# A graph-transformer layer on one core: block counts and the filter pipeline's first products moved within the prologue

## What is computed

```python
xn = _layernorm(x, axis=-1)
x = x + gnn(xn, src, dst, edge_attr_20, edge_weight, edge_attr_3, ...) + attention(xn[None], Wq, Wk, Wv, Wo, bo)[0]
x = x + experts(_layernorm(x, axis=-1)[None], ...)[0]

# gnn, for every edge
xs = x[:, :C] @ (W_in2f_s / sqrt(C));  xv = einsum(x[:, C:], W_in2f_v) / sqrt(C)   # the node table
h = softplus(f_ij @ Wf1 + bf1) - LOG2                                              # f_ij: 20 features of the edge
W = (h @ Wf2 + bf2) * rcut_ij[:, None]                                             # the edge's filter
agg = segment_sum(messages(xs[idx_j], xv[idx_j], direction, W), idx_i)

# attention, 8 heads: softmax over q and k, context = k^T v, out = q context
v = x @ Wv;  q = softmax(x @ Wq);  k = softmax(x @ Wk)
```

## Time and profile before

| | us |
|---|---|
| median of 3 runs | 1355.48 |
| lowest and highest | 1350.85, 1355.99 |
| the profiled execution, its own time | 1353.98 |
| its span | 1352.2 |
| PE, DVE, ACT, POOL busy in the span | 1222.9, 1077.6, 824.4, 846.0 |
| mean granted clock of TensorE | 0.958 of 2.4 GHz |

### The profile page before, as it was taken

How to read it: one execution, slowest core, us unless ns; L and a number is a source line. 1 busy time by engine, 2 the same in 40 slices (tenths; PEclk the granted TensorE clock), 3 DMA queues, 4 the chain that set the end, 5 groups by cost and what they waited for, 6 DMA issues and landing times.

```text
span 1352.2 us, 16153 instructions
## 1 busy us (share of the span) xinstructions
PE 1222.9 (90%) x4175; PEld 709.1 (52%) x4175; DVE 1077.6 (80%) x2018; ACT 824.4 (61%) x1821; POOL 846.0 (63%) x785
## 2 busy tenths in 40 slices
PE   5989999999999998799999999999979999977993
PEld 3566666667776663334343343434434444766870
DVE  5868888899999994788889888898968887577325
ACT  3677777767777641566666666667655774774320
POOL 7167777777777775667676767777675881051215
PEclk8989999999999998899999999999999999978995
DMA  9147776778779857878788888888787881645447
GB/s 267 54 148 274 283 285 233 276 274 307 277 290 340 283 206 276 308 266 288 268 292 280 281 284 283 283 286 299 265 278 249 304 275 38 205 173 167 162 120 231
DMA packets 103663, 336.58 MB, mean 249 GB/s; under 512 B 16260, under 2 KB 17196, under 8 KB 94228
## 3 DMA queue, kind: packets, MB, share of 16 engines
q0 software_dynamic: 56896, 186.92, 39.1%
q1 hardware_dynamic: 46676, 148.63, 31.9%
HBM read 211.34 MB, written 124.14 MB: 248 GB/s over the span
## 4 chain that ended last, share of the span: by engine, by line
PE 63%; DVE 15%; ACT 7%; issue 6%; DMA 5%; POOL 3%; DVEq 1%; SPq 0%; POOLq 0%; ACTq 0%
PE PS L2147 16%; PE PS L2152 13%; PE PS L2083 11%; PE PS L2274 6%; ACT RR L1136 4%; PE PS L1971 3%; PE PS L1961 3%; DVE RR L1627 3%; PE PS L1943 2%; DVE RR L1467 2%; PE PS L2042 2%; DMA RR<-node_table,RR 2%; DVE RR L1647 1%; POOL RR L941 1%; DMA X<-in_x 1%
## 5 line engine op out<-in xcount | busy, mean ns | idle before, releaser
L1136 ACT ACTIVATE RR<-RR 128x256 f32<-128x256 f32 x966 | 394.2, 494 | 245.5 <-PE PS L2152 202.2
L891 POOL DMA_INDIRECT RR<-node_table,RR x322 | 426.0, 1323 | 182.5 <-ACT RR L1136 81.3
L857 POOL DMA_INDIRECT edge_records<-RR x316 | 319.9, 1012 | 115.4 <-issue 67.7
L2147 PE MATMUL PS<-RR 128*125 128x512 f32 x644 | 302.6, 614 | 36.8 <-DVE RR L1627 27.9
L2152 PE MATMUL PS<-RR 128*125 128x512 f32 x644 | 289.6, 592 | 0.0
L2147 PEld LDWEIGHTS PS<-RR 128*125 128x125 f32 x644 | 121.3, 193 | 209.9 <-issue 203.8
L2152 PEld LDWEIGHTS PS<-RR 128*125 128x125 f32 x644 | 120.9, 188 | 155.7 <-issue 155.7
L1467 DVE TENSOR_TENSOR RR<-PS,RR 128x512 f32<-128x512 f32 x237 | 161.0, 686 | 29.9 <-PE PS L2083 28.3
L2083 PE MATMUL PS<-wf_high,h_high 128*128 128x512 f32 x316 | 146.6, 464 | 1.6 <-ACT RR L1090 1.5
L1627 DVE TENSOR_TENSOR RR<-RR 128x1536 f32<-128x1536 f32 (+1 forms) x81 | 140.9, 1740 | 0.0
L2083 PE MATMUL PS<-wf_high,h_low 128*128 128x512 f32 x316 | 125.2, 396 | 0.0
(11 more groups left out here) (340 smaller groups left out, 1828.6 us busy)
## 6 DMA issues: line engine op xcount, KB each, us to landing
RR<-edge_records SPq DMA_DIRECT2D x73, 1040.0 KB, 6.2
expert_inputs<-RR SPq DMA_DIRECT2D x8, 2560.0 KB, 14.2
RR<-in_L_ffn_beta_w SPq DMA_DIRECT2D x8, 1024.0 KB, 7.2
expert_w_raw<-in_L_ffn_expert_w SPq DMA_DIRECT2D x8, 1024.0 KB, 7.5
expert_outputs<-RR SPq DMA_DIRECT2D x27, 256.0 KB, 2.0
RR<-edge_records SPq DMA_DIRECT2D x10, 520.0 KB, 4.4
edge_records<-RR POOLq DMA_INDIRECT x322, 3.9
RR<-node_table,RR POOLq DMA_INDIRECT x322, 5.0
```

The source lines that it names most:

```text
L857: g.indirect_dma_start(out=rec_dram, out_offset=place, in_=ST[:, j, :], in_offset=None).then_inc(scattered[c], 16)
L891: g.indirect_dma_start(out=GB[:, q % GBS, t, 1:5, :].rearrange("p k n -> p (k n)"), out_offset=None, in_=tab_dram, in_offset=bass.Indirect ...
L1136: last = a.activation(message_slot(q)[:, t, k:k + 5:4, :], GB[:, q % GBS, t, 0:k + 3:k + 2, :], ACT.Copy, scale=record_slot(q)[:, t, 4 * C ...
L2147: te.matmul(PS[0:NT, 2 * (r % PSS), :], OH[:, q % OHS, t, 0:NT], GB[:, q % GBS, t, 1:5, :].rearrange("p k n -> p (k n)"), start=(n == 0), ...
```

## The change

It moves instructions and changes two PSUM banks; no instruction is added or removed.

- DVE: `count_block(1)` and `(2)` stand ahead of the wait for the deviations of tiles 2 and 3, `(3)` and `(4)` a place earlier, `(5)`, `(6)` and `(7)` ahead of the wait for those of tiles 6 to 9, `(8)` and `(9)` between the normalisations of tiles 6, 7 and 8.
- PE: the count products stand behind value product 5 instead of 7 (`COUNT_TILE`). Table product 9 and value products 8 and 9 are taken out of the loop and stand between the filter pipeline's first transposes and first layer. The waits for all copies of the prologue stand where their banks are first used again.
- The bias product L2055 writes bank 5 instead of 3, since bank 3 is still in use by value product 8.
- ACT: the rounding of the weights and the first two `stage_f` come a tile earlier; the copies follow PE's new order, and `log_part(0, 0)` stands ahead of the copy of value product 9.
- DVE at the head of the loop: `low(0, 0)` stands ahead of `hidden(0, 1)`.

```diff
@@ -582,7 +582,7 @@
 
             return 4 * (t % 2)
 
-        COUNT_TILE = 7
+        COUNT_TILE = 5
         TILE_STEP, PER = 3, 6
         CTX_STEP = TILE_STEP + PER * NB - 1
         WO_STEP = CTX_STEP + 2
@@ -1024,10 +1024,13 @@
             values(1)
             moments_of((5,))
             later_std(slice(4, 6), 5)
-            for t in range(2, NB):
+            def bias_rows():
+                act.wait_ge(b2_psum, 1)
+                a.activation(b2_rows, PS[:, 5, :], ACT.Copy).then_inc(b2_ready, 1)
+
+            for t in range(2, NB - 1):
                 table_rows(t)
-                if t + 1 < NB:
-                    evac_xT(t + 1)
+                evac_xT(t + 1)
                 if t < 4:
                     moments_of((2 * t + 2, 2 * t + 3))
                 if t == 3:
@@ -1035,8 +1038,9 @@
                     act.wait_ge(nrm_sq, 1)
                     a.activation(inv, ssq, ACT.Sqrt).then_inc(nrm_root, 1)
                     a.preload_act_table_set("natural_log_exp_and_others")
-                values(t)
-                if t == 5:
+                if t < NB - 2:
+                    values(t)
+                if t == 4:
                     act.wait_ge(consts, 3)
                     a.activation(ones2[:, :], two_rows, ACT.Copy)
                     a.activation(ident_r[:, :], ident[:, :], ACT.Copy).then_inc(w_rounded, 1)
@@ -1046,12 +1050,9 @@
                     a.activation(wf2_high[:, :, :], wf2[:, :, :], ACT.Copy).then_inc(w_rounded, 1)
                     stage_f(0)
                     stage_f(1)
-                if t == 7:
+                if t == 6:
                     act.wait_ge(w_ordered, 2)
                     a.activation(b2hl[0:2, :], b2f, ACT.Copy).then_inc(w_rounded, 1)
-
-            act.wait_ge(b2_psum, 1)
-            a.activation(b2_rows, PS[:, 3, :], ACT.Copy).then_inc(b2_ready, 1)
 
             def radial(i, c):
 
@@ -1110,13 +1111,17 @@
                 if 0 <= t < NB and r == 3:
                     exp_k(t)
 
+            bias_rows()
+            table_rows(NB - 1)
             radial(0, 0)
             stage_f(2)
+            values(NB - 2)
+            log_part(0, 0)
             radial(0, 1)
-            log_part(0, 0)
-            log_part(0, 1)
             high(0, 0)
             stage_f(3)
+            values(NB - 1)
+            log_part(0, 1)
             radial(0, 2)
             stage_f(4)
             radial(0, 3)
@@ -1398,21 +1403,26 @@
             dve.wait_ge(edge_in, 16 * 6)
             receiving_blocks()
             count_block(0)
+            count_block(1)
+            count_block(2)
             inverse_root(range(2, 4), 1)
             normal(2)
             normal(3)
-            count_block(1)
-            count_block(2)
+            count_block(3)
             inverse_root(range(4, 6), 2)
             normal(4)
-            count_block(3)
+            count_block(4)
             normal(5)
-            count_block(4)
+            count_block(5)
+            count_block(6)
+            count_block(7)
             inverse_root(range(6, NB), 3)
-            for t in range(5, NB):
-                if t + 1 < NB:
-                    normal(t + 1)
-                count_block(t)
+            normal(6)
+            count_block(8)
+            normal(7)
+            count_block(9)
+            normal(8)
+            normal(9)
             dve.wait_ge(w_rounded, 4)
             stage_f_low(0, 0)
             stage_f_low(0, 1)
@@ -1579,10 +1589,10 @@
 
             stage_f_low(0, 2)
             hidden(0, 0)
-            hidden(0, 1)
-            stage_f_low(0, 3)
             dve.wait_ge(b2_ready, 1)
             low(0, 0)
+            stage_f_low(0, 3)
+            hidden(0, 1)
             stage_f_low(0, 4)
             dve.wait_ge(dirs_ready, 1)
             dve.wait_ge(v_psum, NB)
@@ -1920,9 +1930,8 @@
 
             transpose_x(0)
             transpose_x(1)
-            for t in range(NB):
-                if t == 2:
-                    transpose_x(2)
+
+            def table_product(t):
                 pe.wait_ge(xT_ready, t + 1)
                 if t == 0:
                     pe.wait_ge(wsv_in, 32)
@@ -1933,8 +1942,7 @@
                                      start=True, stop=True)
                 last.then_inc(tab_psum, 1)
 
-                if 2 <= t < NB - 1:
-                    transpose_x(t + 1)
+            def value_product(t):
                 if t == 0:
                     pe.wait_ge(wqkv_in[2], 32)
                 elif t >= 2:
@@ -1943,15 +1951,19 @@
                     last = te.matmul(PS[0:NT, 3 + t % 2, :], XTQ[:, t, k, :], WV[:, k, :], start=(k == 0),
                                      stop=(k == KD - 1))
                 last.then_inc(v_psum, 1)
+
+            for t in range(NB - 1):
+                if t == 2:
+                    transpose_x(2)
+                table_product(t)
+                if t >= 2:
+                    transpose_x(t + 1)
+                if t < NB - 2:
+                    value_product(t)
                 if t == COUNT_TILE:
                     pe.wait_ge(counts_ready, NB)
                     te.matmul(PS[:, 7, 0:NB], ltri[:, :], cnt, start=True, stop=True)
                     te.matmul(PS[:, 7, NB:2 * NB], ones[:, 0:P], cnt, start=True, stop=True).then_inc(counts_psum, 1)
-
-            pe.wait_ge(counts_read, 1)
-            pe.wait_ge(xT_ready, NB)
-            pe.wait_ge(tab_ready, NB)
-            pe.wait_ge(v_ready, NB)
 
             def query(t, k):
                 if k == 0 and t == 0:
@@ -2052,15 +2064,21 @@
 
 
             pe.wait_ge(w_rounded, 5)
-            te.matmul(PS[:, 3, :], ones2[:, :], b2hl[:, :], start=True, stop=True).then_inc(b2_psum, 1)
+            te.matmul(PS[:, 5, :], ones2[:, :], b2hl[:, :], start=True, stop=True).then_inc(b2_psum, 1)
+            table_product(NB - 1)
             transposes(0, 0)
-            transposes(0, 1)
+            value_product(NB - 2)
             pe.wait_ge(wf2_l, 1)
             layer1(0, 0)
+            transposes(0, 1)
+            value_product(NB - 1)
+            pe.wait_ge(tab_ready, NB)
             layer1(0, 1)
             transposes(0, 2)
+            layer1(0, 2)
             transposes(0, 3)
-            layer1(0, 2)
+            pe.wait_ge(counts_read, 1)
+            pe.wait_ge(v_ready, NB)
 
             pe.wait_ge(b2_ready, 1)
             pe.wait_ge(wf2_l, 2)
```

## The result

| | before | changed |
|---|---|---|
| median of 11 runs, us | 1353.2 | 1347.4 |
| lowest and highest, us | 1350.35, 1356.16 | 1338.79, 1350.19 |
| profiled execution: own time, span, us | 1353.98, 1352.2 | 1342.33, 1340.6 |
| mean granted clock | 0.958 | 0.964 |

The ratio of the times is 0.9951, with a 95% interval of 0.993 to 0.9972: 3.8 to 9.5 us less, 6.6 in the middle, against the forecast 3.9. The profiled execution is 11.6 us shorter than the one before, much more than the forecast, so the first question is where in the span these 11.6 us lie.

The account below looks back on a forecast made before the run. PE is busy 90%, but at 70 to 81 us serial ACT and DVE latency leaves it waiting. 4.2 gained less 0.3 for count blocks gives 3.9 us: 1350.1, or 1351.6 against the median; range 1346.5 to 1356.

Parts of the forecast that it names:

- The walk along PE: Prologue tail on PE: one pause of 2.5 us instead of 6.4 in four; step 0 at 75.8, gaining 4.7.
- The step on the clock: Steps 0 and 1: gain 6.4 us if the clock holds through the pause, 4.2 if it falls.
- I take the fall: Pause before step 0: clock assumed to fall, as after three of five similar later pauses; gain 4.2 us.
- Step 0 then costs what it costs today: Step 0 after a clock fall: lasts as before, 7.40 us, instead of about 5.7 at full clock.
- by the same amount: Filter steps behind step 1: POOL's last scatter comes earlier by the whole head start, 4 to 6 us.
- the five pauses behind 590 us: Later PE pauses of 2.57 to 2.67 us: each may lose or keep its clock anew, a fall costing 1.7 us.
- The count blocks: DVE ahead of tile 2: two count blocks fill the 4.59 us wait, delaying it by 0.3 us.
- the slower rival: Count blocks run into POOL before tile 2: PE 6.3 us later, result 1357.6; chance 0.08.
- POOL's slack: Filter steps: 316 scatters need about 400 of 428.70 us, so POOL does not stop the head start.
- The signs: Marks against the forecast: count blocks above 3 us, step 0 later than 77, head start lost by the last filter step.
- The clock holds: Rival: clock stays up through the 2.5 us pause before step 0; 6.1 us less, 1349.4; chance 0.30.
- Given back: Rival: two more clock falls at later pauses take 3.4 of 3.9 us; 1355.0; chance 0.17.

Follow-up runs that it names:

- e4: The changed kernel again, no edit: median 1349.9 us, ratio 0.9962 to the kernel before.
- e6: The changed kernel with count blocks 1 and 2 back behind the normalisations of tiles 2 and 3: 1349.34 us, ratio 0.9978 to the kernel before.
- e7: The changed kernel with the router's small products spread behind three columns of step 1: 1349.6 us, ratio 0.9969 to the kernel before.
- e12: The changed kernel with 22 unread bias products between the fourth transposes and step 0: 1353.6 us, ratio 1.0 to the kernel before.
- e2: The changed kernel with the old DVE order and COUNT_TILE = 7, only the new tail kept: 1349.6 us, ratio 0.9968 to the kernel before.
- e8: The kernel before again, no edit: 1350.9 us, ratio 0.9985 to itself.
- e10: The kernel before a third time, no edit: 1351.36 us, ratio 0.9984 to itself.
- e1: The kernel before with only the change's DVE order and COUNT_TILE = 5: 1350.25 us, ratio 0.9981 to the kernel before.
- e11: The changed kernel with later log parts on ACT, second series: 1347.14 us, ratio 0.9938 to the kernel before.
- e5: The changed kernel with ACT's log parts later, behind the fT copy PE waits for: 1343.36 us, ratio 0.9928 to the kernel before.

## Why the prediction was right

**Where the head start arises.** The walk along PE held to some tenths: table product 9 at 63.31 after a pause of 0.47 (63.0 and 0.5 forecast), one pause of 2.45 (2.5) ended by fT at 75.51 (75.0), step 0 at 76.24 (75.8). The 0.4 by which all is late is table product 8's delay. Step 0 gains 4.3 against 4.7.

**The step on the clock failed in its size.** "I take the fall" was borne out: of six unfilled pauses of this tail the clock fell in four (e4, e6, e7 and e12; not in the changed kernel's first trace nor in e2). "Step 0 then costs what it costs today" was not. Today's 7.40 belong to a pause of 4.23 us: before, the slow clock lasts to about 85.7. Behind 2.45 us it lasted to about 79.3 in e4, and beyond that PE would have waited 0.5 us for ACT's first column anyway (the row at 80.00). Step 0 took 5.99 in e4 and 5.89 where the clock held. The price of the fall at step 1 is 0.7 to 0.8 (21.74 to 21.79 against 21.02 and 21.03), where 2.2 was taken. The price of a slow clock was read from a row with a longer pause in front of it, and from one trace: the old tail gave a step 0 of 6.30 in e8 and 7.11 in e10, too, and the new one 6.48 in e6 and 6.32 in e7 where the clock fell.

**That the head start of step 1 arrives at the last scatter "by the same amount" failed by 1.5 us.** The second fall, behind the router's products, gave back 1.5 in both traces of the changed kernel. It is no effect of the change alone, since e8, the kernel before, has it as well. It was not among the terms, only the five pauses behind 590 us were. These two errors have opposite signs: 6.2 or 5.4 at step 1 (changed, e4) instead of 4.2, less 1.5. That the sum of 3.9 stands near the 4.24 and 3.2 of the last scatter is partly luck.

**The count blocks** cost more than the 0.3 taken. They took 2.81 and 3.15 us against 2.37 in the clear, and nearly all of the excess lies in the mask that begins each, 0.83 and 1.07 in place of the 0.40 of that block. POOL stands beside them with fills and a select; the select is shown with DVE's scan beside it, and behind these rows as it was in the kernel before, where DVE was idle:

```profile
22.01 0.52 POOL L810 MEMSET b_parts<- 128x512 f32 x1
...
22.74 0.81 DVE L1305 TENSOR_TENSOR_SCAN RR<-ones,RR 128x313 f32<-128x313 f32 x1
...
22.81 0.83 POOL L813 TENSOR_SCALAR_AFFINE_SELECT small<-ones 128x64 f32<-128x64 f32 x1
...
24.60 0.52 POOL L821 MEMSET RR<- 128x512 f32 x1
...
25.06 0.53 POOL L822 MEMSET RR<- 128x520 f32 x1
```

```profile
22.52 0.29 POOL L813 TENSOR_SCALAR_AFFINE_SELECT small<-ones 128x64 f32<-128x64 f32 x1
```

The delay of the reciprocal is 1.25 in the mean, and 0.7 arrives at table product 8. That is far from the 6.5 of the slower rival (6.6 by its own numbers, 32.87 less 26.24), and below the 4.2 us from which it decides. The Trainium skill (SBUF — State Buffer, "SBUF: two separate sides") was weighed with a cost of about 2 us for this move; the measured delay of DVE lies between that and the forecast. The prediction used only half of what the section says. It names two kinds of VectorE operation that exclude GpSimd for a whole instruction: those with two SBUF inputs, against GpSimd operations that read SBUF, and those in a 2-port perf mode, against GpSimd operations of any kind. The trace agrees with the first: the select, which reads SBUF, ends 0.09 us behind the scan with its two inputs and takes 0.83 us, 0.29 where DVE was idle. The mask is not of that kind, it has a single input tensor, and the second one, 24.69 to 25.76, ran beside fills alone, which the prediction had taken for harmless. Both masks end 0.17 to 0.18 us behind the end of a fill (22.53 and 25.59), as if they had waited for it; e1, e4 and e11 show the same within 0.01. That would be the second kind, but which mode the mask runs in no trace here shows. The second pair of blocks cost PE nothing: from tile 2's table product to 62 us no idle time stands in its timeline, tile 6 included.

**POOL's slack** held: 428.03 us for the 316 scatters, 428.70 before, and from step 3 to the last scatter 415.59 to 415.71 in every trace but e7's.

**The signs.** Several of the signs that were named did not come out right. The second count block took 3.15 us, more than the 3 that were named, and tile 2's transposes start at 28.78, not within 0.3 of 27.16. Step 0 is later than 77 in e4 (77.45). And of a head start of 5.8 us at step 2 (87.99 against 93.78) 4.2 were left at the last scatter. None of them took the gain away, but the first belongs to a term that was set too low, and the last to one that was missing.

**The rivals.** "The clock holds" describes the changed kernel's first trace up to step 1 (82.13, forecast 81.5), and e2's, but not the rule. "Given back" is real as a mechanism: the later pauses changed sides, three of five fell again. The five are not separate draws: in e4, e5, e8 and e10 groups of 3.67 and 5.37 us alternate. It acts in both directions, and in traces of the same kernel too, so it is spread, and no effect of the change that can be seen. With a rest of 831.6 to 839.8 in 14 traces, one profile against one profile can't tell 4 us.

**The size.** The forecast of 3.9 us lies at the edge of the first series (3.8 to 9.5) and inside the second (0.9946 to 0.9979: 2.8 to 7.3). With the yardstick of e8 and e10 the two come to 4.6 and 3.1.

## What to carry to other kernels

When a pipeline's start-up chain is latency on two engines, put the last throughput work of the stage before into its gaps; then look for what else stands ahead of the copy that the bound engine still waits for, since that order on the other engine gave another 1.3 to 2.0 us at step 1 (e5). Read the price of a clock fall from a pause of the same length as the new one. And before crediting a difference of less than 1% to a change, cut the span at marks and compare several traces of the same kernel: here 7.4 of 11.6 us belonged to the one execution and not to the change.
